# A two-layer network on one core: order of loads, pace of side work and place of the shared blocks

## Chip, cores and metric

The kernel runs on one core of a Trainium2 chip. The metric is the device time of one execution, in microseconds.

## What is computed

The input is x, 8 sequences of 256 tokens with 256 features, all in fp32. Four sublayers follow each other, each with a residual and a layer norm (weights without scale or shift):

```
x = norm(x + attention(x))        # 16 heads of 128, causal
x = norm(x + moe0(x))             # 32 experts, width 96, the 6 best by sigmoid score, weights normalized,
                                  # plus a shared expert of width 192
x = norm(x + ssm(x))              # gated state space layer: in-projection, causal convolution of 4 taps,
                                  # 8 heads of 64, state 64, RMS norm, out-projection
x = norm(x + moe1(x))             # 16 experts, width 176, in 4 groups: the 2 best groups, then the 4 best experts,
                                  # softmax scores, normalized; plus a shared expert of width 352
out = x
```

An expert computes (silu(x Wg) * (x Wu)) Wd for the tokens that chose it, and the results are added with their weights.

## The kernel before

The 2048 tokens are 16 tiles of 128. The tiles are handled in four quads of four tiles (`q`) and in two halves of eight (`h`). The layers of experts are called L0 (moe0) and L1 (moe1). The SSM works on "pairs" `p` of two sequences, which are the same four tiles as a quad.

**The stream.** After attention, everything hangs on one list of blocks, `STREAM` (lines 98 to 108). A block is 128 rows times one expert. Routed blocks (line 95) read rows from a DRAM table `xs`, in which each token's row was scattered to a place sorted by expert; there are 79 of them per half in L0 and 47 in L1, enough for any choice. Shared blocks (line 90) are two per tile and read the rows from SBUF. The list before the change is: L0 shared 0 to 31, L0 half 0 at 32, L0 half 1 at 111, L1 shared of tiles 0 to 7 at 190, L1 half 0 at 206, L1 shared of tiles 8 to 15 at 253, L1 half 1 at 269, the end at 316. Every engine has a loop over n through this list, and places its other work by n, in program order. An engine executes in order, so whatever is placed at n stands in the way of what is placed later.

- TensorE (line 1614): at n it turns the rows of block n+2 (`block_turn`, two transposes of `xb`), does gate and up of block n+1 (`block_gate_up`) and down of block n (`block_down`).
- ScalarE (line 853): copies the turned rows to `xbT` (n+2), silu of the gate (n+1), copies the output of block n to `b_out` (routed) or `acc` (shared).
- VectorE (line 1258): `b_act`, the product of gate and up, of n+1 (line 1111 for L0, 1106 and 1107 for L1), then everything that is not blocks.
- SyncE (line 544): issues loads and stores. `block_load` (line 495) waits until the slot of `bw` is free (a ring of 8 for L0 and 4 for L1, which counts `b_down_done`), issues the weights (line 505), waits until the rows' slot is free (a ring of 4, `xb_turned`), and issues the rows (line 511). It is called for block n+4 in L0 and n+3 in L1. `block_store` (line 513) writes two blocks of `b_out` to the DRAM table `os`, once the second is copied.
- GpSimd: `scatter` (line 611) has one indirect DMA per tile and choice (24 for a quad of L0, 16 for one of L1); `gather` (line 628) has one per choice of a tile (6 or 4) into the ring `og` of two tiles, and waits for the combine of the tile two before. It also multiplies `mix` for the SSM (line 644) and adds squares (line 650).

**Slots.** The SSM for the tokens of one half, and the choosing of L1's experts, run beside the blocks of the next stretch. `SPAN` (line 156) has two stretches of the stream: L0 half 1 (79 blocks), and L1 shared plus L1 half 0 (63 blocks). `slots_at` (line 159) spreads 90 slots v evenly over each. Pair i of the stretch starts at slot `FRONT[i]`, and a step of its plan has a number o = v - FRONT[i]: norm statistics at -3, turning of the normalized tile for pair 0 at -2, projections from 0, head products at 15 to 29 (they wait for `mix`, line 1545), out-projection at 33 and 35, gating of L1 at 43, choice at 44, its rank at 45, places at 46, scatter at 48; the table of block rows for the half at 48 and 49 of pair 1.

**Gathering and combining.** L0's result of a half is gathered and added to x in the next stretch: tile j at slots 0 to 4 and 13 to 28 (`mix_slot`, `gather_slot`, lines 167 to 174). `combine` (line 1088) adds the shared part and then one scaled row per choice (line 1095). It must be done before the norm of its quad. L1's half 0 is combined during L1's half 1 (`tail_mix`, line 180); half 1 is combined after the last block (lines 1348 to 1353), each quad followed by its norm and its store.

**Weighing.** `weights` (line 1050) computes for a quad the normalized weights (lines 1063 to 1067), the rows to gather (1070 to 1076), and the weight of each choice (1079 to 1085), in one piece of VectorE's program.

## Time and profile before

| what | value |
|---|---|
| runs | 1993.6, 1988.36, 1995.99 us; median 1993.6 |
| profiled execution | 1995.88 us, span 1994.2 us |
| granted TensorE clock, mean | 0.876 |
| PE busy | 1511.0 us (76%) |
| DVE, ACT, POOL busy | 975.6, 759.6, 442.1 us |
| DMA | 331.71 MB, mean 166 GB/s |

The span is the time from the first to the last instruction in the profiled execution; what lies around it is 1.7 us. Busy times are sums over the whole span, and they hide that the kernel has stages with different limits: attention until about 670, the shared blocks of L0 until 786, L0's first half until 954, its second half with the SSM of pairs 0 and 1 until 1284, L1's shared blocks and first half with pairs 2 and 3 until 1664, shared blocks until 1734, L1's second half until 1932, and the tail. The stages were told apart by VectorE's `b_act` instructions, one for each block. A wait is put down to the engine whose event came last; "issue" and "remote" (on the chain: "another core or an unknown queue") mean that the profile shows nothing that was waited for.

### The profile page before, as it was taken

Reading aid. Unit: us, or ns where it says so; the run is one execution under the profiler, and the core shown is the slowest. Engines: PE = TensorE matmul, PEld = TensorE weight load, DVE = VectorE, ACT = ScalarE, POOL = GpSimd, SP = SyncE. Lnnn points to the kernel's source line nnn. Section 1 sums busy time; section 2 is a strip of 40 time slices with the busy share of each in tenths; the row PEclk is TensorE's granted clock in tenths of the full one; section 3 lists DMA queues with packets and bytes.
Section 4 is the critical chain, followed back from the end, with each engine's and each line's share of the span. In section 5 each row is a group of like instructions: output and inputs, shape, how many; then the busy total and the mean of one; then the engine's idle time right before and its main releaser. Section 6 shows DMA issues by size and latency. Waiting matters only on the chain.

```text
span 1994.2 us, 30357 instructions
## 1 busy us (share of the span) xinstructions
PE 1511.0 (76%) x9344; PEld 1256.6 (63%) x9344; DVE 975.6 (49%) x3299; ACT 759.6 (38%) x2327; POOL 442.1 (22%) x422
## 2 busy tenths in 40 slices
PE   7999999999973418788457977827898787877760
PEld 6998898898873317667336766615666565655540
DVE  5777777777773302411336562425855333243315
ACT  5565565555530104345243543304344232223320
POOL 1010100000006470000515134261511503122015
PEclk9999999999986658799779988868998897888885
DMA  8265256246002142699637575421755664177743
GB/s 314 113 244 188 71 225 241 69 173 242 1 1 92 59 146 60 201 301 309 210 119 252 165 219 187 141 82 60 244 164 183 219 196 144 59 251 229 229 154 94
DMA packets 173078, 331.71 MB, mean 166 GB/s; under 512 B 17280, under 2 KB 85888, under 8 KB 171680
## 3 DMA queue, kind: packets, MB, share of 16 engines
q1 hardware_dynamic: 157600, 288.31, 43.4%
q0 software_dynamic: 15360, 41.96, 6.5%
q8 instruction: 58, 0.95, 0.2%
q14 instruction: 60, 0.49, 0.1%
HBM read 196.41 MB, written 133.27 MB: 165 GB/s over the span
## 4 chain that ended last, share of the span: by engine, by line
PE 45%; DVE 15%; issue 10%; DMA 8%; another core or an unknown queue 8%; ACT 7%; POOL 4%; SPq 2%; DVEq 0%; ACTq 0%; POOLq 0%
PE psum L407 37%; DMA xb<-xs 8%; PE psum L1579 2%; POOL xs L618 2%; POOL og L633 2%; PE psum L1401 1%; ACT p_sb L730 1%; DVE x L1095 1%; PE psum L1550 1%; SPq L505 1%; DVE s_sb L1123 1%; PE psum L1412 1%; DVE stats L940 1%; ACT p_sb L728 1%
## 5 line engine op out<-in xcount | busy, mean ns | idle before, releaser
L407 PE MATMUL psum<-xbT,bw 128*96 128x128 f32 (+1 forms) x2392 | 338.6, 293 | 0.0
L407 PEld LDWEIGHTS psum<-xbT,bw 128*96 128x96 f32 (+1 forms) x2392 | 312.8, 194 | 0.6 <-issue 0.3
L633 POOL DMA_INDIRECT og<-l_os,l_back_of x160 | 161.4, 1009 | 575.0 <-DMA l_os<-b_out 310.1
L407 PE MATMUL psum<-bw,b_act 96*128 96x256 f32 (+2 forms) x692 | 229.1, 424 | 63.9 <-ACT b_out L803 20.0
L1111 DVE TENSOR_TENSOR b_act<-psum,b_gated 96x128 f32<-96x128 f32 x190 | 53.9, 286 | 370.4 <-ACT b_gated L790 338.5
L618 POOL DMA_INDIRECT xs<-x,row_of x160 | 159.9, 1000 | 236.3 <-DVE row_of L1026 189.4
L1106 DVE TENSOR_TENSOR b_act<-psum,b_gated 128x128 f32<-128x128 f32 x126 | 36.7, 291 | 343.0 <-ACT b_gated L787 298.4
L779 ACT ACTIVATE xbT<-psum 128x256 f32<-128x256 f32 x252 | 96.3, 382 | 249.1 <-PE psum L1579 230.1
L407 PEld LDWEIGHTS psum<-bw,b_act 96*128 96x128 f32 (+2 forms) x692 | 113.6, 206 | 103.5 <-issue 75.9
L407 PE MATMUL psum<-l_shared_w,b_act 128*128 128x256 f32 (+1 forms) x192 | 70.9, 467 | 128.4 <-DVE b_act L1111 50.1
L1579 PE MATMUL psum<-ident,xb 128*128 128x128 f32 x504 | 110.2, 302 | 75.6 <-DMA xb<-xs 71.1
L1579 PEld LDWEIGHTS psum<-ident,xb 128*128 128x128 f32 x504 | 64.7, 151 | 140.4 <-DMA xb<-xs 101.8
L583 POOL TENSOR_TENSOR aw_lo<-aw_raw,aw_hi 128x512 fp32r<-128x512 f32 x32 | 41.2, 1289 | 484.0 <-ACT aw_hi L696 484.0
L803 ACT ACTIVATE b_out<-psum 128x256 f32<-128x256 f32 x252 | 96.8, 384 | 130.7 <-PE psum L407 125.8
L728 ACT ACTIVATE p_sb<-s_sb,neg_max 128x128 f32<-128x128 f32 x128 | 51.7, 404 | 210.8 <-DVE neg_max L1123 210.8
L790 ACT ACTIVATE b_gated<-psum 96x128 f32<-96x128 f32 x190 | 51.9, 274 | 194.1 <-PE psum L407 101.8
L407 PEld LDWEIGHTS psum<-l_shared_w,b_act 128*128 128x128 f32 (+1 forms) x192 | 34.1, 222 | 145.0 <-issue 58.5
L786 ACT ACTIVATE b_gated<-psum 128x128 f32<-128x128 f32 x126 | 35.0, 277 | 231.2 <-PE psum L407 181.8
L1095 DVE SCALAR_TENSOR_TENSOR x<-og,l_mix_of,x 128x256 f32<-128x256 f32 x160 | 79.7, 498 | 67.6 <-DMA og<-l_os,l_back_of 61.5
L407 PE MATMUL psum<-xT_hi,aw_hi 128*128 128x512 f32 x256 | 103.5, 404 | 10.5 <-POOL aw_lo L583 10.2
L407 PE MATMUL psum<-xT,l_shared_w 128*128 128x128 f32 (+1 forms) x640 | 102.2, 317 | 0.0
L407 PE MATMUL psum<-xT_hi,aw_lo 128*128 128x512 f32 x256 | 101.6, 397 | 0.0
(217 smaller groups left out, 3706.8 us busy)
## 6 DMA issues: line engine op xcount, KB each, us to landing
xs<-zeros SPq DMA_DIRECT2D x42, 1792.0 KB, 17.3
bw<-l_w SPq DMA_DIRECT2D x94, 640.0 KB
bw<-l_w SPq DMA_DIRECT2D x158, 320.0 KB
xb<-xs SPq DMA_DIRECT2D x252, 128.0 KB
l_os<-b_out SPq DMA_DIRECT2D x124, 256.0 KB
decay_all<-decay_dram SPq DMA_DIRECT2D x32, 384.0 KB
aw_raw<-attn_w SPq DMA_DIRECT2D x8, 1024.0 KB, 6.9
xs<-x,row_of POOLq DMA_INDIRECT x160
```

Of the source, the lines that this page charges most:

```text
L407: last = nc.tensor.matmul(out_ap, w, m, start=start and n == 0, stop=stop and n == len(pairs) - 1, **kw)
L583: pool.tensor_tensor(aw_lo[:, w], aw_raw[:, w], aw_hi[:, w].bitcast(F32), ALU.subtract).then_inc(aw_split, 1)
L618: pool.indirect_dma_start(xs[q // 2], bass.IndirectOffsetOnAxis(ap=row_of[:, t, k:k + 1], axis=0), x[:, t, :], None) \
L633: pool.indirect_dma_start(og[:, i % MIX_RING, k, :], None, os[f["layer"]][t // HALF_TILES], bass.IndirectOffsetOnAxis(ap=back_of[f["layer" ...
L728: act.activation(p_sb[:, u % 3, 0:P], s_sb[:, u % 2, 0:P], ACT.Exp, bias=neg_max[:, u % 3, 0:1], scale=-1.0, accum_out=row_sum[:, u % 3, 0:1])
L779: act.activation(xbT[:, r % 2].rearrange("p c t -> p (c t)"), psum[:, TURN_BANK, 0:DC * BLOCK], ACT.Copy).then_inc(xbT_ready, 1)
L790: act.activation(b_gated[h, n % 2, 0, :], psum[h, gu_bank(n), 0:P], ACT.Silu).then_inc(b_gated_ready, 1)
L803: act.activation(to, psum[:, DOWN_BANK, 0:D], ACT.Copy).then_inc(b_copied, 1)
L1095: ins = dve.scalar_tensor_tensor(x[:, t, :], og[:, i % MIX_RING, k, :], mix_of[f["layer"]][:, t, k:k + 1], x[:, t, :], ALU.mult, ALU.add)
L1106: dve.tensor_tensor(b_act[:, n % 2, 0, :], psum[:, gu_bank(n), P:2 * P], b_gated[:, n % 2, 0, :], ALU.mult)
L1111: dve.tensor_tensor(b_act[h, n % 2, 0, :], psum[h, gu_bank(n), P:2 * P], b_gated[h, n % 2, 0, :], ALU.mult).then_inc(bt_ready, 1)
L1579: last = pe.transpose(psum[:, TURN_BANK, c * BLOCK:(c + 1) * BLOCK], xb[:, r % XB_RING, c * P:(c + 1) * P], ident[:])
```

## The change

- **Loads.** `block_load` is cut in two. `LOADS` says at which n each is issued: weights for block n+6 in L0 and n+3 in L1, rows for block n+6, with exceptions at the start of a half. At one n, rows stand before weights, and both before the store. Sizes and numbers of the rings stay.
- **Slots.** 102 slots in place of 90, the pairs start at 18 and 50 in place of 8 and 40, and the second stretch ends 8 blocks before L1's second half (55 blocks). Gathers of L0 are placed two per slot, `combine` of L0 in two parts of three choices, in slots of their own; the scatter of L1 for pairs 0 and 2 is placed one DMA per slot (16 slots), for pairs 1 and 3 it stays in one piece. The steps of choosing L1's experts are placed in slots of their own (choice 45, rank 46, places 47, and for the table 48 to 51).
- **Weighing** is cut into three functions at three consecutive blocks.
- **The last 16 shared blocks** of L1 stand at the end of the stream. The new list is: L1 half 0 at 206, L1 half 1 at 253 (`TAIL`), L1 shared of tiles 8 to 15 at 300 to 315. L1's half 0 is combined at TAIL + 8 + 5j, tiles 8 to 11 of half 1 at the shared blocks 5, 8, 10 and 12; tiles 12 to 15 after the last block as before.

The operations themselves, their number and their shapes stay the same. Cut to what matters:

```diff
@@ the stream and its slots
-    if _f is L1:
-        FIRST["shared", _h] = len(STREAM)
-        STREAM += shared_blocks(L1, range(HALF_TILES * _h, HALF_TILES * (_h + 1)))
+    if (_f, _h) == (L1, 0):
+        FIRST["shared", 0] = len(STREAM)
+        STREAM += shared_blocks(L1, range(HALF_TILES))
     FIRST[_f["layer"], _h] = len(STREAM)
     STREAM += routed_blocks(_f, _h)
+FIRST["shared", 1] = len(STREAM)
+STREAM += shared_blocks(L1, range(HALF_TILES, TILES))
...
-FRONT = 8, 40
-SLOTS = 90
-SPAN = (FIRST[0, 1], FIRST["shared", 0]), (FIRST["shared", 0], FIRST["shared", 1])
+FRONT = 18, 50
+SLOTS = 102
+SPAN = (FIRST[0, 1], FIRST["shared", 0]), (FIRST["shared", 0], FIRST[1, 1] - 8)
...
-def mix_slot(j):
-    return 1 + j if j < QUAD else 16 + 4 * (j - QUAD)
-def gather_slot(j):
-    return max(0, mix_slot(j) - (1 if j < QUAD else 3))
+GATHERED = 0, 3, 6, 9, 18, 21, 27, 31
+COMBINED = (4, 5), (7, 8), (10, 11), (13, 14), (25, 26), (28, 29), (32, 34), (37, 38)
...
-    return TAIL + 2 + 4 * j
+    return TAIL + 8 + 5 * j if j < HALF_TILES else FIRST["shared", 1] + (5, 8, 10, 12)[j - HALF_TILES]
+
+def load_at(n):
+    f, h, m, _ = STREAM[n]
+    first = FIRST[f["layer"], h]
+    if f is L0:
+        weights = first - 5 if h == 0 and m < L0_RING - 1 else n - 6
+    else:
+        weights = first - 5 if h == 0 and m < L1_RING else n - 3
+    return weights, max(n - 6, first - 4 + m // 2)
+
+LOADS = {}
+for _n in ROUTED:
+    for _kind, _at in zip(("weights", "rows"), load_at(_n)):
+        LOADS.setdefault(_at, []).append((_kind, _n))
+
+def weigh_at(f, q):
+    return FIRST[0, 0] + 4 + 4 * q if f is L0 else TAIL + (1, 4, 10, 15)[q]
@@ SyncE: block_load is cut into weights_load (row, wait for the slot, bw) and rows_load (wait for the ring, xb)
-            for n in range(-4, BLOCKS + 1):
-                for lead, f in ((4, L0), (3, L1)):
-                    if 0 <= n + lead < BLOCKS and is_routed(n + lead) and STREAM[n + lead][0] is f:
-                        block_load(n + lead)
+            for n in range(BLOCKS + 1):
+                for kind, b in LOADS.get(n, ()):
+                    if kind == "rows":
+                        rows_load(b)
+                for kind, b in LOADS.get(n, ()):
+                    if kind == "weights":
+                        weights_load(b)
...
-                    if n == tail_mix(QUAD * q + 6):
+                    if n == tail_mix(QUAD * q + 3) + 5:
                         store(q)
@@ GpSimd: scatter takes a part, gather a range of k
-                        if v == gather_slot(j):
-                            gather(L0, HALF_TILES * h + j)
+                        if 0 <= v - GATHERED[j] < 3:
+                            k = 2 * (v - GATHERED[j])
+                            gather(L0, HALF_TILES * h + j, (k, k + 1))
...
-                        if o == 48:
+                        if i == 0 and 48 <= o < 64:
+                            scatter(L1, p, o - 48)
+                        if i and o == 48:
                             scatter(L1, p)
-                if n == TAIL:
+                if n == tail_mix(0) - 3:
                     all_stored(L1, 0)
                 for j in range(HALF_TILES):
-                    if n == tail_mix(j) - 2:
-                        gather(L1, j)
+                    if n == tail_mix(j) - 3:
+                        gather(L1, j, range(L1["top"]))
@@ VectorE: weights is cut into weights_sum, rows_back, weights_of; combine takes a range of k
-                for q in range(QUADS):
-                    if n == FIRST[0, 0] + 4 + 4 * q:
-                        weights(L0, q)
-                    if n == (FIRST["shared", 1] + 2 + 4 * q if q < 2 else TAIL + 4 * q):
-                        weights(L1, q)
+                for f in LAYERS:
+                    for q in range(QUADS):
+                        if n == weigh_at(f, q):
+                            weights_sum(f, q)
+                        if n == weigh_at(f, q) + 1:
+                            rows_back(f, q)
+                        if n == weigh_at(f, q) + 2:
+                            weights_of(f, q)
...
-                        if v == mix_slot(j):
-                            combine(L0, HALF_TILES * h + j)
+                        for part in range(2):
+                            if v == COMBINED[j][part]:
+                                combine(L0, HALF_TILES * h + j, range(3 * part, 3 * part + 3))
...
                             gate_read(L1, p)
                             gate_groups(L1, p)
+                        if o == 45:
                             choose(L1, p)
-                        if o == 46:
+                        if o == 47:
                             slots(L1, p)
-                        if i and o == 48:
+                        if i and o == 49:
                             table(L1, h)
-                        if i and o == 49:
+                        if i and o == 51:
                             rows_read(L1, h)
...
-                for j in range(HALF_TILES):
+                for j in range(HALF_TILES + QUAD):
                     if n == tail_mix(j):
-                        combine(L1, j)
+                        combine(L1, j, range(L1["top"]))
...
             for q in range(2, QUADS):
-                for t in range(QUAD * q, QUAD * (q + 1)):
-                    combine(L1, t)
+                if q == QUADS - 1:
+                    for t in range(QUAD * q, QUAD * (q + 1)):
+                        combine(L1, t, range(L1["top"]))
@@ TensorE
-                        if o == 45:
+                        if o == 46:
                             rank(L1, p)
-                        if i and o == 47:
+                        if i and o == 48:
                             count(L1, h)
-                        if i and o == 49:
+                        if i and o == 50:
                             rows_turn(L1, h)
```

## Rows read from the trace of the kernel before

**Rows 1.** The page's chain that ended last, shares of the span by engine

```profile
PE 45%; DVE 15%; issue 10%; DMA 8%; another core or an unknown queue 8%; ACT 7%; POOL 4%; SPq 2%; DVEq 0%; ACTq 0%; POOLq 0%
```

**Rows 2.** Windows: busy us (instructions) by engine, granted clock, DMA share, GB/s

```profile
794.00:844.00 50.00, 34.94 (x196) 31.03 (x196) 26.65 (x101) 15.87 (x50) 0.00 (x0) 0.80 0.64 204
844.00:954.00 110.00, 93.09 (x685) 78.48 (x684) 16.40 (x58) 56.46 (x172) 0.00 (x0) 1.00 0.94 303
954.00:1018.00 64.00, 20.96 (x106) 16.85 (x106) 20.28 (x60) 7.89 (x24) 34.92 (x36) 0.62 0.54 169
1018.00:1284.00 266.00, 216.22 (x1262) 171.28 (x1261) 137.56 (x375) 119.84 (x286) 73.41 (x51) 0.92 0.60 188
1284.00:1356.00 72.00, 24.77 (x101) 17.97 (x100) 24.23 (x75) 4.58 (x16) 47.17 (x49) 0.61 0.31 95
1356.00:1664.00 308.00, 265.57 (x1425) 194.03 (x1424) 160.42 (x418) 119.41 (x286) 72.00 (x55) 0.92 0.54 175
1664.00:1734.00 70.00, 54.47 (x278) 39.98 (x277) 20.74 (x93) 13.19 (x45) 21.63 (x23) 0.83 0.29 95
1734.00:1932.00 198.00, 148.99 (x825) 111.97 (x823) 64.93 (x228) 59.78 (x184) 22.74 (x24) 0.89 0.69 222
1932.00:1994.20 62.20, 1.30 (x4) 0.59 (x4) 29.30 (x88) 0.62 (x2) 31.32 (x32) 0.52 0.30 91
```

**Rows 3.** Waits of PE, 1734 to 1932: total us, times, longest us

```profile
PE psum L1579 <- DMA xb<-xs: 47.8, 30, 3.4
```

**Rows 4.** The page's DMA issues: count, KB each

```profile
bw<-l_w SPq DMA_DIRECT2D x158, 320.0 KB
xb<-xs SPq DMA_DIRECT2D x252, 128.0 KB
l_os<-b_out SPq DMA_DIRECT2D x124, 256.0 KB
```

**Rows 5.** Waits of PE, 794 to 844

```profile
PE psum L407 <- DVE b_act L1111: 13.9, 4, 3.8
```

**Rows 6.** Groups of DVE, 794 to 844: busy us, mean ns, idle before them

```profile
L1083 DVE TENSOR_TENSOR hits<-hits,weight 128x192 f32<-128x192 f32 x16 | 4.7, 352 | 0.1
L1079 DVE TENSOR_TENSOR hits<-place,places 128x192 f32<-128x192 f32 x16 | 4.6, 351 | 0.0
L1111 DVE TENSOR_TENSOR b_act<-psum,b_gated 96x128 f32<-96x128 f32 x17 | 4.5, 285 | 23.1 <-ACT b_gated L790 23.0
L1085 DVE TENSOR_REDUCE l_mix_of<-hits 128x24 f32<-128x768 f32 x4 | 3.8, 953 | 0.1
```

**Rows 7.** Groups of POOL, 954 to 1018

```profile
L633 POOL DMA_INDIRECT og<-l_os,l_back_of x36 | 34.9, 970 | 224.8 <-DMA l_os<-b_out 214.1 <-issue 10.7
```

**Rows 8.** Timeline of DVE: start us, us, instruction, idle before

```profile
969.22 3.09 DVE L1095 SCALAR_TENSOR_TENSOR x<-og,l_mix_of,x 128x256 f32<-128x256 f32 x6 [9.51 <-DMA og<-l_os,l_back_of]
```

**Rows 9.** Timeline of ACT, two of its pauses in bursts of POOL

```profile
1009.57 0.28 ACT L790 ACTIVATE b_gated<-psum 96x128 f32<-96x128 f32 x1 [19.97 <-remote]
...
1685.15 0.28 ACT L786 ACTIVATE b_gated<-psum 128x128 f32<-128x128 f32 x1 [12.25 <-remote]
```

**Rows 10.** Waits of PE, 1018 to 1284

```profile
PE psum L1550 <- POOL mix L648: 20.7, 2, 16.0
```

**Rows 11.** Waits of PE, 1356 to 1664

```profile
PE psum L1550 <- POOL mix L648: 12.5, 1, 12.5
...
PE psum L1579 <- DMA xb<-xs: 5.6, 6, 2.2
```

**Rows 12.** Timeline of POOL, a gather among DVE's scans

```profile
1072.04 2.26 POOL L633 DMA_INDIRECT og<-l_os,l_back_of  x1
```

**Rows 13.** Timeline of ACT, the last routed block's copy

```profile
1933.71 0.38 ACT L803 ACTIVATE b_out<-psum 128x256 f32<-128x256 f32 x1 [1.48 <-PE psum L407]
```

**Rows 14.** Timeline of DVE in the tail, first tile combined

```profile
1943.89 2.05 DVE L1095 SCALAR_TENSOR_TENSOR x<-og,l_mix_of,x 128x256 f32<-128x256 f32 x4 [11.46 <-DMA og<-l_os,l_back_of]
```

**Rows 15.** Timeline of DVE in the tail, last layer norm

```profile
1985.18 1.41 DVE L940 BATCH_NORM_STATS2 stats<-x 128x6 f32<-128x256 f32 x4
```

More of the change, by code:

```diff
@@ L609, in _, with scatter @@
             low_part(GROUPS - 1, 3)
[L611 to L619 removed]
+            def scatter(f, q, part=None):
+                if part in (None, 0):
+                    if f["layer"] == 0 and q == 0:
+                        pool.wait_ge(xs_zeroed, 16 * ZEROED * (GROUPS - 1))
+                    pool.wait_ge(placed, QUADS * f["layer"] + q + 1)
+                rows = [(t, k) for t in range(QUAD * q, QUAD * (q + 1)) for k in range(f["top"])]
+                for t, k in rows if part is None else rows[part:part + 1]:
+                    pool.indirect_dma_start(xs[q // 2], bass.IndirectOffsetOnAxis(ap=row_of[:, t, k:k + 1], axis=0), x[:, t, :], None) \
+                        .then_inc(scattered[q], 16)
             def all_stored(f, h):
@@ L626, in all_stored, with gather @@
                 pool.wait_ge(weighed, QUADS * f["layer"] + 2 * h + 2)
-            def gather(f, t):
+            def gather(f, t, ks):
                 i = f["layer"] * TILES + t
-                wait(pool, combined, i - MIX_RING + 1)
-                for k in range(f["top"]):
+                if ks[0] == 0:
+                    wait(pool, combined, i - MIX_RING + 1)
+                for k in ks:
                     pool.indirect_dma_start(og[:, i % MIX_RING, k, :], None, os[f["layer"]][t // HALF_TILES],
@@ L1097, in combine @@
                         chained(ins)
[L1098 to L1099 removed]
+                if ks[-1] == f["top"] - 1:
+                    ins.then_inc(combined, 1)
+                    dve.wait_ge(combined, i + 1)
             def block_act(n):
```

54 lines of the change are left out of this document (30 added, 24 removed).

## The prediction

> **What bounds it now.** I read the chain of waits first, then the span cut into the kernel's own stages, then who waits in each. On the chain PE has 45%, and 18% lies with "issue" and an unnamed queue [rows 1]: the kernel is PE-bound in places and idles in others. The stages say where [rows 2]. L0's first routed half has a start (794 to 844, DMA share 0.64) and a steady part (844 to 954: 58 blocks, one DVE instruction each, so 1.90 us a block, at DMA share 0.94 and 303 GB/s). The two state-space stretches each open with a hole, 954 to 1018 (PE busy 21 of 64) and 1284 to 1356 (25 of 72), and then run at a PE share of 0.81 and 0.86. L1's second routed half takes 198 us with PE busy 149, and 47.8 of the 49 idle microseconds are waits for `xb` [rows 3]. The 16 shared blocks ahead of it take 70 us, and after its last block PE does nothing for 60 us while gathers and combining run.
>
> **Rows ahead of weights.** Before, `xb` of block n+3 (L1) or n+4 (L0) is issued right behind the same block's weights. For L1 it is issued when down(n-1) has ended and wanted by the turn after down(n): one block of lead. After, rows are asked for 6 blocks early, bounded by the ring of four, so when turn(n+2) is done: four blocks of lead. Weights of L1 keep their lead of 3, but now stand behind the wait for that turn and one more DMA issue, some 1 us later. They are wanted two blocks on. A cycle of 198/46 = 4.3 us with one block of lead says that asking, landing and turning take about 4.3 us; (4.3 + 1)/2 = 2.7 us a block is then what weights allow, under what PE needs (149/46 = 3.2, part of it at the lower clock). The stage moves 198 x 222 = 44 MB, 145 us at 303 GB/s. So PE's 149 plus 7 for the two layer norms and for weighing that moves into this stage: 156, **-42**. Ends: -49 (no idle left), and -12 if weights take over most of the wait.
> In L0's first half the queue has little to give. 794 to 954 moves 10.2 + 33.3 = 43.5 MB [rows 2], 576 KB a block [rows 4]. At 303 GB/s that is 144 us, at the rate of a full share (303/0.94 = 322) 135; I take 141 of 160, **-19**, of which the earlier rows give the few us above 303 GB/s and the next part the rest. By the Trainium skill (DMA: Bandwidth & Descriptors, Specifications) one core's HBM limit is some 358 GB/s, by which an estimate would be 122 us; the trace disagrees, since a share of 0.94 gives 303.
>
> **Choosing in parts.** Weighing of a quad of L0 held DVE and cost PE 13.9 us in four waits [rows 5], and then some blocks at a lower clock. In three parts the longest is the last, (4.6 + 4.7 + 3.8)/4 = 3.3 us [rows 6]; DVE has 23.1/17 = 1.4 us free a block and one block of lead, so about 1 us of wait is left a quad. That lets DMA set the pace from 794 on: counted above.
>
> **The two openings.** SSM work of slot FRONT-2 needs four tiles combined and normalized. POOL issues a gather per (34.9 + 10.7)/36 = 1.27 us [rows 7]; the first tile is on DVE at 969.22 [rows 8], the next each six gathers (7.6 us) later, so the fourth is there at 992. Nothing in the change makes that faster: POOL doesn't wait for slots. What changes is what PE does beneath. Turning for pair 0 moves from slot 6 of 90 over 79 blocks (the 6th or 7th block) to slot 16 of 102 (the 13th): six more blocks at PE 93/58 = 1.6 us are done in the hole, 10 us. Splitting `combine` lets a block's b_act between the halves, and the chain reaches its end some 7 us earlier: **-17**. In the second opening the turn goes from the 4th block to the 9th: 5 shared blocks of 2.8 us (54.5 us busy at clock 0.83 is 45 at full, over 16) are 14, and 3 for the split: **-17**. Ends for both together: 0 and -60 (half of 43 + 47 idle, and all of what ACT loses below). In these bursts of POOL's indirect DMAs ACT stands idle with no releaser named, 19.97 us in one piece [rows 9]. Since the 36 gathers stay in one run, I leave those stalls where they are.
>
> **Scatter in parts.** Pair 0 and pair 2 scatter 16 times in a row, and PE waits for a `mix` behind them: 16.0 us and 12.5 us at the longest [rows 10, 11]. One scatter a slot leaves a mix waiting for one at most: **-15 and -14**. Against it: beside DVE's scans an indirect DMA took 2.26 us [rows 12], against 0.97 alone [rows 7], and 16 of those are 21 us more of POOL, spread over 16 slots of about 3 us, where it is idle two thirds of the time; no charge. The Trainium skill (SBUF, State Buffer; "two separate sides") says that GpSimd and DVE take a shared port pair as an exclusive lock, so that scatters amid DVE work would lengthen; the trace agrees, 2.26 against 0.97. Rows earlier in the L1 stage between 1356 and 1664: 5.6 us of `xb` waits [rows 11], **-5**; at best all the 42 us that PE idles there, at worst nothing.
>
> **More slots.** 102 slots over 79 and 55 blocks pack the same SSM work into fewer blocks, 1.29 and 1.85 slots a block instead of 1.14 and 1.43. The steps of choosing (rank, places, table) get slots of their own and are waited for by PE as before; I take nothing for them, under the blocks between. PE's work is the same and no DMA load is near its limit there (shares 0.60 and 0.54), so nothing, if PE is the limit. If it is not, see the last rival.
>
> **Shared blocks at the end.** Before: 70 + 62.2 = 132.2 us for the shared stage and the tail. After: L1's second routed half follows its own choosing directly. That ends 8 blocks ahead of block 253 (25 us), against 16 scatters at 1.27 (20 us) and their landing; SP's queue stands at block 249 until then, with weights of 252 and a store behind it. It fits by 2 us. What doesn't go is the stall in the burst, 12.25 us [rows 9]: **+12** kept. Tail, from the last routed copy at 1933.7: four gathers and their landing bring the first tile at 1943.9, +10 [rows 13, 14]. Combining stands at shared blocks 5, 8, 10, 12, that is at +15, +23, +30, +36 with 2.5 us each; the ring of two lets the gathers of tiles 12 and 13 go by +44. The 16 shared blocks end at +45. Then layer norm 5.6, tiles 12 and 13 (2.5 each) to +56; tile 14's gathers wait for tile 12's combine: 5 + 2.3, and tile 15's end 5 later, +64; combine 2.5 and the last norm with its store, 9.0 (1985.18 to the end [rows 15]): +76.5. In sum 12 + 1.7 + 76.5 = 90, **-42**. Bounds: -54 without the stall, -15 if the scatters cover nothing (12 more) and shared blocks are slowed by combining (15).
>
> **Sum.** -42 - 19 - 17 - 17 - 15 - 14 - 5 - 42 = -171. The profiled execution took 1995.9 us (span 1994.2), 2.3 above the median of the three runs: 1995.9 - 171 = 1825, set against the median 1993.6 - 171 = 1823. I say 1824.
>
> **Rivals.**
> - *Weights take over the wait* (0.14). Same queue, ring of four unchanged. For: PE then waits at gate-up where it waited at the turn, and L0 is at its DMA limit already. Against: two blocks of lead against one. L1's half gives 12 in place of 42, L0's first 8 in place of 19: 1824 + 41 = 1865.
> - *The openings stay as they are* (0.10). The chain gathers, combine, norm is as long as before, and the unnamed stalls of ACT fall on the added blocks: 34 lost, and a second such stall of 12 at block 249: 1870.
> - *The stalls without a releaser go too* (0.05): openings -50 in place of -34, no 12 at the scatter, L1 at -49: 1789.
> - *A slot has a price of its own* (0.03), slower. If DVE, ACT and POOL hand-offs set the time of a slot, not PE's work, the two stretches cost 330/90 = 3.67 and 380/90 = 4.22 us a slot, and 102 of each are 374 + 431, plus 8 bare blocks of 3.3: 831 in place of 710. With -42 - 19 - 42 elsewhere that is 2012. It decides above 3.86 us a slot; mine need 3.0. Against: PE is busy 0.81 and 0.86 behind the openings.
> - *Nothing comes of it* (0.02): SP, with rows standing before weights, waits for turns where it used to run ahead, and gives back at block 249 (252's weights) and in the SSM stretches what the turns gain: 1990.
>
> **Numbers.** The forecast has 0.66. All cases but the last two are faster: 0.95; same 0.02; slower 0.03 (0.5%, 10 us, is about what a measurement of this kernel tells from no change). The range holds the forecast with its own spread (about 25 either way), the first two rivals and most of the third: 1785 to 1880.
>
> **What would show it.** Waits of the turn for `xb` near nothing, and the DMA share in L1's second half near 0.9, with 3.3 us a block; if gate-up (`xbT,bw`) waits for weights there, the first rival holds. PE waits for `mix` of more than 3 us gone. Thirteen blocks done before pair 0's first turn. In the tail, under 35 us from the last shared block to the end. Wrong would be a slot of 3.9 us, or a hole of over 20 us at block 253.

## The result and the profile after

The changed kernel takes 1852.2 us, the median of four runs (1845.9 to 1856.4); beside it the kernel before took 1994.8 (four runs). The ratio is 0.9285, 95% interval 0.9247 to 0.9323: 143 us less, against 171 forecast, and inside the range. The sign and the order of size were right, and so were most terms; the openings, and the slots that were put at nothing, were not, and they make most of the 28 us that are missing.

From the top of the changed kernel's page: the span, the busy sums, and PE's and its clock's tenths in 40 slices:

```profile
span 1848.6 us, 30360 instructions
...
PE 1493.5 (81%) x9344; PEld 1240.5 (67%) x9344; DVE 995.6 (54%) x3299; ACT 751.7 (41%) x2326; POOL 448.7 (24%) x422
...
PE   7999999999997342688856888984689998798992
...
PEclk9999999999998655799987999995799999899996
```

PE's busy sum is nearly unchanged (1493.5 against 1511.0): the gain is idle time of PE. Where it went shows in the kernel's own stages. Windows of the changed kernel; they answer to [rows 2]:

```profile
core 0: us, PE busy (x) PEld busy (x) DVE busy (x) ACT busy (x) POOL busy (x), PEclk, DMA share, GB/s
794.00:936.00 142.00, 121.58 (x900) 108.12 (x899) 42.73 (x160) 66.83 (x225) 0.00 (x0) 1.00 0.96 313
936.00:1000.00 64.00, 34.72 (x180) 29.24 (x179) 22.14 (x67) 14.27 (x45) 35.16 (x36) 0.72 0.70 216
1000.00:1242.00 242.00, 207.83 (x1193) 160.24 (x1193) 150.00 (x380) 113.47 (x266) 78.23 (x54) 0.95 0.63 193
1242.00:1315.00 73.00, 33.74 (x148) 23.94 (x148) 19.63 (x51) 6.25 (x22) 41.05 (x44) 0.68 0.37 119
1315.00:1600.00 285.00, 245.17 (x1311) 179.06 (x1311) 171.51 (x438) 113.21 (x266) 93.84 (x72) 0.93 0.59 182
1612.00:1769.00 157.00, 140.29 (x842) 102.95 (x840) 74.44 (x280) 59.80 (x186) 30.39 (x32) 0.97 0.88 292
1769.00:1817.00 48.00, 42.27 (x244) 30.81 (x242) 18.19 (x51) 11.29 (x38) 23.17 (x24) 0.93 0.27 80
1817.00:1848.60 31.60, 2.37 (x4) 1.00 (x4) 19.90 (x69) 0.38 (x1) 7.88 (x8) 0.50 0.21 67
```

The steady part of L0's first half now moves 313 GB/s at a share of 0.96. The first opening (936 to 1000) has PE busy 35 of 64 us where it was 21. The second (1242 to 1315) has hardly changed: 34 of 73 against 25 of 72. L1's second routed half (1612 to 1769) took 157 us with PE busy 140, at a granted clock of 0.97, where it had 198 and 149. From the last routed block to the end are 48 + 32 us.

Who PE waits for in L1's second half, as in [rows 3]:

```profile
engine line waited for: us in total, times, longest us
PE psum L426 <- issue: 7.0, 13, 1.5
PE psum L426 <- ACT xbT L815: 5.1, 7, 1.1
PE psum L426 <- DVE b_act L1155: 4.5, 2, 2.7
```

`xb` is gone from the list, and no wait for weights stands in its place. For the second opening the same view names something else:

```profile
PE psum L426 <- ACT acc L839: 33.0, 2, 21.4
PE psum L426 <- issue: 6.2, 2, 4.9
```

I cut each trace by the times of `b_act`, of which every block has one, so that a stage is the same work in every kernel. Two columns (runs 9 and 10 explain them) are from another chip:

```
stage, us (by b_act)        before  after | before  after | forecast
                            the chips     | a chip with-  |
                            shown so far  | out pauses    |
L0 shared blocks             115.4  125.2 |  62.1   61.2  |    0
L0 half 0                    169.0  148.3 | 167.1  150.1  |  -19
L0 half 1 + SSM 0,1          330.4  305.4 | 315.1  293.9  |  -17 -15
L1 shared 0-7 (opening)      123.2  115.5 | 111.8   94.6  |  -17
L1 half 0 + SSM 2,3          256.5  254.9 | 253.8  249.8  |  -14 -5 +12
L1 half 1                    198.1  156.7 | 202.0  162.4  |  -42
L1 shared 8-15                67.6   48.1 |  49.8   41.4  |  } -54
tail                          62.5   31.6 |  61.5   31.7  |  }
```

### The profile page after: what moved, and what is told of

It is laid out like the page before. It is cut to its first block, busy times and chain, and to the rows that moved or that the text cites. A ratio compares the mean times of both kernels' runs of the same rounds, so it can differ in the third digit from the quotient of the medians.

```text
span 1848.6 us, 30360 instructions
## 1 busy us (share of the span) xinstructions
PE 1493.5 (81%) x9344; PEld 1240.5 (67%) x9344; DVE 995.6 (54%) x3299; ACT 751.7 (41%) x2326; POOL 448.7 (24%) x422
## 4 chain that ended last, share of the span: by engine, by line
PE 49%; DVE 17%; another core or an unknown queue 10%; issue 9%; ACT 7%; DMA 5%; POOL 2%; SPq 1%; DVEq 0%; ACTq 0%; POOLq 0%
PE psum L426 40%; DMA l_os<-b_out 4%; PE psum L1633 2%; DVE x L1142 2%; PE psum L1455 2%; ACT p_sb L766 1%; DVE s_sb L1171 1%; PE psum L1604 1%; PE psum L1466 1%; DVE conv L1256 1%; DVE stats L976 1%; DVE x L990 1%; ACT p_sb L764 1%; ACT kT_hi L742 1%
## 5 line engine op out<-in xcount | busy, mean ns | idle before, releaser
L426 PE MATMUL psum<-xbT,bw 128*96 128x128 f32 (+1 forms) x2392 | 325.7, 285 | 13.0 <-issue 6.8
L426 PEld LDWEIGHTS psum<-xbT,bw 128*96 128x96 f32 (+1 forms) x2392 | 298.5, 186 | 18.9 <-issue 11.2
L426 PE MATMUL psum<-bw,b_act 96*128 96x256 f32 (+2 forms) x692 | 222.6, 413 | 72.3 <-ACT b_out L839 27.1
L650 POOL DMA_INDIRECT xs<-x,row_of x160 | 165.6, 1035 | 221.0 <-DVE row_of L1062 176.3
L426 PEld LDWEIGHTS psum<-bw,b_act 96*128 96x128 f32 (+2 forms) x692 | 107.8, 196 | 115.5 <-issue 74.8
L1633 PE MATMUL psum<-ident,xb 128*128 128x128 f32 x504 | 106.1, 293 | 5.6 <-ACT xbT L815 4.7
L1142 DVE SCALAR_TENSOR_TENSOR x<-og,l_mix_of,x 128x256 f32<-128x256 f32 x160 | 87.5, 547 | 27.4 <-DMA og<-l_os,l_back_of 22.2
L426 PEld LDWEIGHTS psum<-xT,l_shared_w 128*128 128x128 f32 (+1 forms) x640 | 92.7, 212 | 13.4 <-issue 10.8
## 6 DMA issues: line engine op xcount, KB each, us to landing
xs<-zeros SPq DMA_DIRECT2D x42, 1792.0 KB, 17.4
```

The lines of the kernel that those rows point to most:

```text
L426: last = nc.tensor.matmul(out_ap, w, m, start=start and n == 0, stop=stop and n == len(pairs) - 1, **kw)
L650: pool.indirect_dma_start(xs[q // 2], bass.IndirectOffsetOnAxis(ap=row_of[:, t, k:k + 1], axis=0), x[:, t, :], None) \
L1142: ins = dve.scalar_tensor_tensor(x[:, t, :], og[:, i % MIX_RING, k, :], mix_of[f["layer"]][:, t, k:k + 1], x[:, t, :], ALU.mult, ALU.add)
L1633: last = pe.transpose(psum[:, TURN_BANK, c * BLOCK:(c + 1) * BLOCK], xb[:, r % XB_RING, c * P:(c + 1) * P], ident[:])
```

## The experiments

The first four runs shared a chip; the changed kernel's 1852.2 us is the time to hold them against. It was measured beside a kernel before of 1994.8 us and these beside 1998.5, so some 4 us of every such difference of totals are open; the stages don't depend on it. Behind each median stands in brackets that of the kernel before on the same chip.

**1. Loads issued as before.** `LOADS` is not used; both loads of a block stand together, weights first.

```diff
-                for kind, b in LOADS.get(n, ()):
-                    if kind == "rows":
-                        rows_load(b)
-                for kind, b in LOADS.get(n, ()):
-                    if kind == "weights":
-                        weights_load(b)
+                for lead, f in ((4, L0), (3, L1)):
+                    b = n + lead
+                    if b < BLOCKS and is_routed(b) and STREAM[b][0] is f:
+                        weights_load(b)
+                        rows_load(b)
```

> The changed kernel with the loads placed as before: block n+4 (L0) and n+3 (L1), weights and right behind them the rows. Theory (rows asked for one block ahead of their use set the pace of L1's half, and a part of L0's first half): L1's second half goes from 157 us back to about 198, L0's first half from 148 to about 155, together +50: about 1900 us against 1852 of the changed kernel. Rival (the gain of those stages comes from other edits, such as the shared blocks leaving and weighing in parts): within 10 us of 1852.

Measured: 1918.6 us (1998.5), ratio 0.957 (0.953 to 0.962), so this part alone is worth some 66 us. L1's second half is 211.8 us, L1's first half 268.6 (+14), L0's first half 154.8 (+6.5). PE's wait for `xb` in L1's second half, 1629 to 1840:

```profile
PE psum L1632 <- DMA xb<-xs: 47.4, 30, 3.4
```

The 47.8 us of `xb` of [rows 3] are back, as 47.4. The half costs more than in the kernel before (211.8 against 198.1) although these waits are the same: PE is busy 155.6 us in it, at a granted clock of 0.87, against 149.3 at 0.89, and it has 8.6 us of other waits. It also holds the weighing of quads 0 and 1 now; the two layer norms were in it before. In L1's first half the waits for `xb` are 14.3 us, in seven, against 5.6 in the kernel before [rows 11], and that is the loss of 14 us. That PE comes to the turns at other times with 102 slots in 55 blocks may be why they are longer; it wasn't tested.

**2. Rows after weights, with the lead kept.** The two loops over `LOADS` change places.

> The changed kernel with the order at each block turned round: weights first, then rows; the rows are still asked for six blocks early. Theory (it is the lead that counts, four blocks in place of one, and not which of the two goes first): within 8 us of 1852. Rival (rows that stand behind weights land late whatever the lead): waits for xb come back in L1's second half and the time is 1870 to 1890.

Measured: 1843.3 us (1998.5), ratio 0.922 (0.919 to 0.926); the changed kernel's is 0.9285. The lead counts, and the order named first in the change is no gain: the other way round is 9 us faster, most of it in L0's first half (139.9 against 148.3). I had allowed 8 us either way. In the windows of that half the queue is fuller with weights first: 336 GB/s at a share of 0.99 (794 to 927), where the changed kernel has 313 at 0.96. Why the order does that isn't known.

**3. Shared blocks 8 to 15 back in front of L1's second half.** The rest as changed; combining of the second half falls behind the last block again, and the slots end 8 blocks ahead of the shared blocks.

```diff
-    if (_f, _h) == (L1, 0):
+    if _f is L1:
...
-FIRST["shared", 1] = len(STREAM)
-STREAM += shared_blocks(L1, range(HALF_TILES, TILES))
```

> The changed kernel with L1's shared blocks of tiles 8 to 15 back ahead of L1's second half, and tiles 8 to 11 combined after the last block. Theory (the shared blocks cover the tail's gathers at the end, and cover little in the middle): +45 us, 1897. Rival (in the middle they cover the scatter and its stalls, so that the gain is half of that): +25, 1877.

Measured: 1877.1 us (1998.5), ratio 0.939 (0.937 to 0.942), 25 us more. The rival had the number. The tail is 62.9 us again, +31; but the shared blocks take 41.9 us in the middle where the kernel before needed 67.6. The choosing ends 8 blocks before them, as in the changed kernel, so the burst of scatters and its pause fall on the routed blocks ahead. Of what the move and the earlier choosing give together, 25 is the move.

**4. Scatter of pairs 0 and 2 in one piece.**

```diff
-                        if i == 0 and 48 <= o < 64:
-                            scatter(L1, p, o - 48)
-                        if i and o == 48:
+                        if o == 48:
                             scatter(L1, p)
```

> The changed kernel with L1's scatters of pairs 0 and 2 in one piece of 16 again. Theory (PE waits for mix behind them, 16 and 12.5 us): a wait of PE for POOL's mix of 12 to 16 us comes back in each of the two stretches, +29, 1881. Rival (the wait is only moved, and in one piece the scatters cost less of POOL): within 8 us of 1852.

Measured: 1887.3 us (1998.5), ratio 0.945 (0.941 to 0.950): 35 us more, 20 in L0's second half, 16 in L1's first. PE's waits there, 940 to 1260 and then 1376 to 1648:

```profile
PE psum L1602 <- POOL mix L681: 19.4, 2, 17.8
...
PE psum L1602 <- POOL mix L681: 19.1, 2, 17.4
```

17.8 and 17.4 us in one piece, where the kernel before had 16.0 and 12.5 [rows 10, 11]. The term stands, and was a little too small. The charge that the prediction named and left out, 21 us of POOL for 16 scatters beside DVE's scans, came as 5 and 6: three of each 16 took 2.25 to 2.28 us, and the 16 together 20.5 and 21.6 us in the changed kernel, where 16 undisturbed ones take 15.4.

Runs 5 to 8 came on another chip, on which the kernel before took 1854.5 us, not 1995, and runs 9 to 11 on a third with 1843.0. So between chips I compare ratios and stages, not times. The changed kernel itself didn't run beside runs 5 to 8; put together from the stages that they leave alone, it would take 1706 us there.

**5. Weighing in one piece again** (`weights_sum`, `rows_back` and `weights_of` of a quad at one n; in L1 too, whose second half took 158.0 us, as in runs 7 and 8).

> L0's weighing of a quad back in one piece, its blocks as in the changed kernel. My theory (weighing held DVE, and PE beneath it, by 13.9 us in four waits [rows 5], and with rows ahead DMA sets the pace of that stage): the start of L0's first routed half is up to 12 us longer, 1852 + 5 to 12. Rival (DMA alone sets the stage's pace, share 0.96 in the changed kernel's trace, so a wait of PE for DVE is given back at once): within 3 us of 1852.

Measured: 1716.6 us (1854.5), ratio 0.9265 (0.923 to 0.930). L0's first half took 163.7 us; in the two other kernels on the same chip that leave it as changed (runs 6 and 7) it took 152.5 and 151.9, so 11 to 12 less. PE's waits for `b_act` here, 678 to 842, and in the changed kernel (run 9), 681 to 831:

```profile
PE psum L426 <- DVE b_act L1159: 14.1, 4, 4.0
```
```profile
PE psum L426 <- DVE b_act L1159: 1.9, 4, 0.8
```

14.1 us in four waits is the 13.9 of [rows 5]. They are not given back, although DMA's share is 0.95 over the half. About half of the loss is PE's clock: it is busy 136.0 us in the half at a granted 0.94, and 129.4 at 1.00 in run 7. By the ratios alone the loss doesn't show: 0.9265 here, 0.9246 for the changed kernel in run 9, each within the other's interval; it rests on the stage. With run 1's 6.5 that makes some 18 of this half's 17 to 21 us: one third is the loads, two thirds the weighing in parts.

**6. The openings as before** (FRONT 8, 40; SLOTS 92; six gathers of a tile in one slot, `combine` in one slot).

> The shape of both openings as before (8 and 40 slots in front, 92 slots, a tile's gathers and its combine in one slot), the rest as in the changed kernel. If the openings gave what I forecast (17 each): 1852 + 34 = 1886. Rival (only the first opening gave anything; in the second the hole stayed, 142 us to the first turn of pair 2 less what the first opening gave): 1852 + 8 to 17, 1860 to 1869, with L1's shared blocks 0 to 7 and first half as long as in the changed kernel to 5 us.

Measured: 1731.1 us (1854.5), ratio 0.933 (0.930 to 0.937). Against the kernels on the same chip that leave these stages as changed (runs 5 and 8), L0's second half is 300.4 us to their 297.8 and 296.0, and the L1 stretch 115.2 + 242.2 = 357.4 to their 343.7 and 344.6. So the openings are worth 3 to 4 and 13 us, 17 of the 34 forecast. (The total is 25 above the 1706: 7 more lie in L1's second half, 164.5 us against 158, where the waits are no longer but PE is busy 145.2 us at a granted 0.93 against 137.6 at 0.98. Whether that has to do with the openings isn't shown; the changed kernel has 162.4 us there in run 9, at 0.96.) The rival of this run was wrong too: the second opening does gain, and more than the first, on a chip where nothing pauses.

**7. Pair 1's scatter later.** It stood at its slot 48, with 16 DMAs ahead of the second opening's gathers.

```diff
+                    if h and v == 12:
+                        scatter(L1, 1)
...
-                        if i and o == 48:
+                        if p == 3 and o == 48:
                             scatter(L1, p)
```

> The scatter of pair 1 in L1's opening (28 DMAs of POOL in a row with the gathers behind it) is moved behind the first four gathers of the choosing. Theory A (the second opening ends when the gathers of pair 2 are through POOL's queue, 16 scatters of 1.27 us ahead of them are 20 us, and their burst holds the signals of PE): first turn of pair 2 up to 20 us earlier, 1832 to 1845. Theory B (the hole is PE's late signals in any burst, and POOL's queue is not the bound): the pauses only move, within 4 us of 1852.

Measured: 1694.7 us (1854.5), ratio 0.914 (0.912 to 0.917). The opening's stage took 82.4 us against 94.6 in runs 5 and 8, and L1's first half 245.6 against 249.1 and 250.0. That is theory A: POOL's queue holds the second opening. It gave 12 there, of the up to 20 us expected.

**8. L0's scatters of quads 2 and 3 spread over the first routed half.**

```diff
-            for q in range(QUADS):
+            for q in range(2):
                 scatter(L0, q)
...
+            for j in range(2 * QUAD * L0["top"]):
+                q, part = 2 + j // (QUAD * L0["top"]), j % (QUAD * L0["top"])
+                pool.wait_ge(b_down_done, 12 + 19 * j // 10 + 1)
+                scatter(L0, q, part)
```

> L0's scatters of quads 2 and 3 (48 of 96 in one run, under L0's first routed half) are spread, one for every 1.9 blocks from block 12 on. Theory A (what PE's increments of semaphores wait for is a dense run of POOL's indirect DMAs; ACT's unnamed pauses of 12.5, 21.3 and 24.9 us between 690 and 754 are waits for those): the pauses in that stretch go, L0's first routed half is 148 - 30 = 118 us by PE's blocks, but DMA's share of 0.96 allows less: some 135, so 1815 to 1840. Theory B (the pauses have to do with the number of indirect DMAs, or with the DMA load, not their density): pauses stay, spread over the half, within 5 us of 1852 or slower.

Measured: 1705.4 us (1854.5), ratio 0.918 (0.915 to 0.922). This says nothing on its question: the trace of this chip holds no pause that it could have taken away. L0's first half took 156.1 us where runs 6 and 7 took 152: spreading costs 4 where nothing pauses. What it would do on a chip with pauses stays open.

**9 and 10. The changed kernel and the kernel before, once more.**

> The changed kernel once more, unaltered, beside the kernel before. The last four kernels ran on a chip where the kernel before takes 1854 us and their traces hold no pause without a releaser over 4 us. Theory (the pauses belong to the chip, or to its condition, and the change's parts have their price without them): on such a chip 1706, put together from stages that those four left as they were; on one like the first, 1852. Rival (the pauses come and go from run to run on one chip): times that differ by over 50 us within this kernel's own runs.

> The kernel before once more, for its trace. Theory (pauses belong to the chip): on a chip that takes 1854 us the trace holds none of ACT's unnamed pauses of 12 to 25 us, and the 140 us less than 1994 lie within runs of POOL's indirect DMAs: about 56 in L0's shared stage (as 62 against 125 us in the other kernels), the rest in L0's first half, the two openings and the scatters; stages without such runs are as long as before to 3 us. Rival (a slower chip throughout, the clock or the memory): the difference is spread over all stages in proportion, 7% each.

Measured: 1705.4 us for the changed kernel (1843.0), ratio 0.9246 (0.918 to 0.931), and 1843.2 for the kernel before in its one profiled run. 1706 had been put together from stages. The kernel before took 1994.8, 1998.5 and (in the last run below) 1998.9 on some chips and 1854.5 and 1843.0 on others, and on each chip its runs agree to 25 us. Its stages without pauses stand in the table above: up to L0's shared blocks 618.3 us against 671.3 (-53), in them 62.1 against 115.4 (-53), L0's second half -15, the second opening -11, shared 8 to 15 -18; L0's first half -2, L1's first and second half -3 and +4, tail -1. Nearly all of the 152 us lies in stages in which POOL issues indirect DMAs in long runs, as expected; it is not spread. The first 53 are the end of attention, which the expectation didn't name: L0's scatters begin there, at 603.

**11. Weights first and pair 1's scatter late, together.**

> Weights of a step asked for before its rows (their lead kept), and pair 1's scatter behind the first four gathers of the second opening. If both gains stand and add: 9 for the order and 16 for the later scatter (12 in the opening, 4 in the blocks before it): 25 below the changed kernel, 1681 on a chip without the pauses, 1827 on one with them. Rival (the scatter only moves its cost behind the opening, and the order is worth nothing outside one chip): within 5 us of the changed kernel.

Measured on the same chip as 9: 1674.8 us (1843.0), ratio 0.907 (0.902 to 0.913), against 1705.4: 31 us less than the changed kernel. The opening's stage is 82.1, L1's first half 243.8, L0's first half 145.5, L1's second half 155.1. In the changed kernel beside it these took 94.6, 249.8, 150.1 and 162.4. Both gains stand. It is the fastest kernel of the study, on a chip without pauses; on one with them it was not run.

**12. On top of that, the opening's combines 3 to 4 slots later.** In the timeline of DVE in the first opening of the changed kernel (run 9), DVE comes to the first combine long before the rows:

```profile
839.10 0.29 DVE L1159 TENSOR_TENSOR b_act<-psum,b_gated 96x128 f32<-96x128 f32 x1 [1.24 <-ACT b_gated L826]
839.30 0.41 DVE L1139 TENSOR_TENSOR x<-x,acc 128x256 f32<-128x256 f32 x1
849.66 1.55 DVE L1142 SCALAR_TENSOR_TENSOR x<-og,l_mix_of,x 128x256 f32<-128x256 f32 x3 [9.94 <-DMA og<-l_os,l_back_of]
851.24 0.29 DVE L1159 TENSOR_TENSOR b_act<-psum,b_gated 96x128 f32<-96x128 f32 x1
```

9.94 us idle at the head of the queue, and the `b_act` of the blocks behind it wait with it; PE waits 9.8 us for one of them.

```diff
-FRONT = 18, 50
-SLOTS = 102
+FRONT = 22, 54
+SLOTS = 106
...
-GATHERED = 0, 3, 6, 9, 18, 21, 27, 31
-COMBINED = (4, 5), (7, 8), (10, 11), (13, 14), (25, 26), (28, 29), (32, 34), (37, 38)
+GATHERED = 0, 3, 6, 9, 22, 25, 31, 35
+COMBINED = (7, 8), (11, 12), (14, 15), (17, 18), (29, 30), (32, 33), (36, 38), (41, 42)
```

> On top of the last kernel (weights first, pair 1's scatter later), the combining of an opening's first four tiles stands 3 to 4 slots later and SSM work 4 slots later (FRONT 22, 54; 106 slots), the gathers where they are. In both traces of the changed kernel DVE reaches the first combine 10 us (second opening 14 us) before its rows have landed, with the b_act of two blocks queued behind it, and PE waits for those: the split of combine didn't help there. Theory (blocks held behind the first combine are what is left of the opening): PE's longest wait for b_act in each opening falls from 9.8 and 14 us to under 5, and the time by 5 in each, 10 in all: a ratio to the kernel before of 0.902 where 0.9074 was measured, 1665 on a chip without the pauses. Rival (the chain gathers, combine, norm sets the end of the hole, and blocks done in it are missed as cover later, where slots come denser, 106 in the same blocks): within 4 us of the last kernel, with PE's wait moved from b_act to x or to the steps behind it.

Measured: 1859.5 us (1998.9), ratio 0.9285 (0.922 to 0.935), on a chip with pauses, so neither number of the expectation can be held against it. By stages against run 2, which has the same order of loads on such a chip: L0's second half is 296.7 us against 305.6, of which run 7 would give 4 to 5 to pair 1's scatter. PE's longest wait for `b_act` in that opening is 4.0, under the 5 of the theory, but run 2 has 1.1 there, so on such a chip it shows nothing. And the opening and the half behind it took 396.5 us against 370.6, and PE's longest wait in 1235 to 1360 is this:

```profile
PE psum L1490 <- DVE x L992: 31.5, 1, 31.5
```

31.5 us for the last tile's x: PE's wait has moved, as the rival has it, and become longer. But not by the rival's cause. DVE has combined the fourth tile by 1275.2, and then stands at a block's `b_act`, which waits for ACT's silu, with the norm queued behind it; timelines of DVE and ACT:

```profile
1272.12 3.12 DVE L1144 SCALAR_TENSOR_TENSOR x<-og,l_mix_of,x 128x256 f32<-128x256 f32 x6
1305.34 0.29 DVE L1156 TENSOR_TENSOR b_act<-psum,b_gated 128x128 f32<-128x128 f32 x1 [30.10 <-ACT b_gated L825]
```
```profile
1304.70 0.28 ACT L824 ACTIVATE b_gated<-psum 128x128 f32<-128x128 f32 x1 [26.92 <-remote]
```

So PE's wait is one of the pauses of the next section, and the number says nothing on the later combines. It begins in a run of 40 indirect DMAs (1249 to 1300), of which 16 are the scatter that run 11 moved there too. What run 11 would give with pauses, and run 12 without, stays open.

## What the pauses are

The unnamed stalls of ACT [rows 9] were the one thing that I could only keep or drop in the sum. In the changed kernel the second opening begins so; timeline of ACT, 1236 to 1275, then of PE:

```profile
1241.41 0.39 ACT L839 ACTIVATE b_out<-psum 128x256 f32<-128x256 f32 x1
1249.44 0.28 ACT L822 ACTIVATE b_gated<-psum 128x128 f32<-128x128 f32 x1 [7.65 <-remote]
...
1271.88 0.28 ACT L822 ACTIVATE b_gated<-psum 128x128 f32<-128x128 f32 x1 [21.88 <-remote]
```
```profile
1250.69 2.37 PE L426 MATMUL psum<-l_shared_w,b_act 128*128 128x256 f32 x4 [4.88 <-issue]
1252.99 2.93 PE L426 MATMUL psum<-xT,l_shared_w 128*128 128x128 f32 x12
```

PE's last gate-up starts at 1252.99 and takes 2.93 us. ACT, which waits here for one semaphore, moved by PE, takes it up at 1271.88, 16 us later. The same place in the changed kernel on a chip without pauses (there it begins at 1124):

```profile
1124.00 0.38 ACT L839 ACTIVATE b_out<-psum 128x256 f32<-128x256 f32 x1
1126.03 0.28 ACT L822 ACTIVATE b_gated<-psum 128x128 f32<-128x128 f32 x1 [1.64 <-PE psum L426]
...
1128.62 0.28 ACT L822 ACTIVATE b_gated<-psum 128x128 f32<-128x128 f32 x1 [2.04 <-PE psum L426]
...
1131.22 0.28 ACT L822 ACTIVATE b_gated<-psum 128x128 f32<-128x128 f32 x1 [1.15 <-PE psum L426]
```

Two shared blocks follow in steps of 2.6 us, and each time ACT's releaser is PE. The same can be asked of all 316 blocks: how long after the end of PE's gate-up, and of ACT's own instruction before it, does ACT start on that block? In the trace of the kernel before it is over 2 us in 11 blocks, 129 us in all, and in that of the changed kernel in 18 blocks, 167 us; every one of these delays begins inside a run of 8 or more indirect DMAs or less than 1 us behind it. In the traces of both kernels on the other kind of chip (runs 9 and 10) no block has one, though the runs of DMAs are just as long and dense (96 from 604 to 727 us, 1.28 us each). From ACT's silu to DVE's `b_act` no delay over 2 us stands in any of the four. So in these traces the pauses come only in such runs, and only on some chips. The records of semaphores are incomplete in the traces with pauses (DVE's `b_act` has 293 for 316 blocks in the kernel before), so they can't say where PE's signal was held up. What differs between the chips is not shown.

## Why the prediction was right, and where not

Where not said otherwise the numbers are those without pauses (right half of the table), since they show the parts clean; the total is nearly the same on both kinds of chip (137 and 143 us).

- *Rows ahead, L1's second half*: -42 forecast, -39.6 and -41.4 measured. Right, and by its own mechanism: no `xb` and no weights in PE's waits. That the stage's 156 came as 157 (on the chips of the forecast) is in part luck: PE was busy 140 and idle 17, where I had 149 and 7. The clock was granted at 0.97, 0.89 before [rows 2], and the time was lost again in short waits for ACT and unnamed ones. The 7 were also given for the wrong reason in part: the two layer norms stood in this half before, only the weighing moved in.
- *L0's first half*: -19, measured -17 and -21. Right, and in its parts too: I had given the loads the few us above 303 GB/s and the weighing the rest, and the runs put 6.5 on the loads and 11 to 12 on the weighing. My ends for the rate, 303 and 322 GB/s, held on the chips of the forecast (313 at a share of 0.96) but not as a rule: run 2 moved 336 there at 0.99, and without pauses the changed kernel moved 333 over the whole half at 0.99, so 303/0.94 was not the rate of a full share.
- *Scatter in parts*: -15 and -14; alone 20 and 16 (run 4). Right, a little small.
- *First opening*: -17, and 3 to 4 by undoing it. What failed is the step on splitting `combine`, which was to let a block's `b_act` between the halves and end the chain 7 us earlier. The blocks more in the hole came: 15 stand ahead of pair 0's first turn instead of 8, and PE's idle in the 64 us fell from 32 to 22. But the turn comes no earlier, 49.8 us after the half's first block against 47.6 before. DVE stands 9.94 us with the first half of the first combine at the head of its queue, as it stood 9.51 with the whole of it [rows 8], and no block gets past; and what the hole gives, the slots behind it give back in part (below).
- *Second opening*: -17. Without pauses the stage gave -17.2. With them it gave -7.7, since pauses took 11 us of that stage before (123.2 - 111.8) and 21 after (115.5 - 94.6): more blocks stand in the burst, and each needs PE's signals. That is what the rival "openings stay as they are" said of it, and it was right for that opening, on those chips. My text left those stalls where they are, and that was the step that failed there.
- *More slots: nothing.* This was the term mis-sized most, by some 15 us: L1's first half had -14 and -5 due, and gave -4. The waits of PE over the shared and routed blocks of this stretch, kernel before and changed one, without pauses:

```profile
PE psum L407 <- DVE b_act L1107: 27.9, 4, 14.6
PE psum L1434 <- DVE x L954: 15.2, 3, 11.3
PE psum L1550 <- POOL mix L648: 12.7, 2, 12.4
PE psum L407 <- DVE prefix L1007: 7.1, 2, 5.0
...
PE psum L1579 <- DMA xb<-xs: 4.5, 6, 2.5
...
PE psum L407 <- issue: 1.0, 1, 1.0
PE psum L1550 <- DVE y L1238: 1.0, 1, 1.0
```
```profile
PE psum L426 <- DVE b_act L1155: 19.0, 4, 14.0
PE psum L1488 <- DVE x L990: 12.5, 4, 6.9
PE psum L426 <- issue: 8.0, 6, 3.1
PE psum L1604 <- DVE y L1286: 6.3, 5, 2.1
...
PE psum L1588 <- DVE h_tok L1269: 3.6, 2, 2.2
PE psum L426 <- DVE prefix L1043: 1.4, 2, 1.2
PE psum L1604 <- POOL mix L681: 1.0, 1, 1.0
...
PE psum L1633 <- DMA xb<-xs: 0.6, 1, 0.6
```

`mix`, `prefix`, `xb` and `b_act` fell by 12, 6, 4 and 9 us; but waits for `y`, `h_tok` and unnamed ones rose from 2 to 18. I put this down to the same SSM work standing in 55 blocks in place of 63, which leaves PE less to do between a step and what it needs from DVE; no run gave the 8 blocks back alone, so that is argued, not shown. "Nothing, if PE is the limit" held the condition, and it isn't quite: PE is busy 0.89 there. The rival "a slot has a price" named the mechanism, and was wrong by far in size: at 3.4 us a slot, even with the 8 blocks without slots counted in ((94.6 + 249.8)/102), it stayed under the 3.86 at which it decides.
- *Shared blocks at the end* (-42): on the chips of the forecast the stretch from the last routed block took 79.7 us (48.1 + 31.6); I had 78.2 (76.5 and 1.7; the terms of the 76.5 as written add up to 75.5). The stall of 12 at the scatter burst came as 9.5, from 1578.9 to 1588.4, and in L1's first half. Right on both. Run 3 adds what the sum didn't separate: only 25 of the 50 us are the move's, the rest is the choosing's earlier end.

Of the rivals, weights didn't take over the wait, and "nothing comes of it" fell with every run. "The stalls go too" asked for the change to remove them; a chip did that, and the gain was no larger for it (137).

The sum by undoing parts one at a time is 66 + 35 + 17 + 25 + 12 = 155 against 143. It mixes totals with pauses and stages without them, so 12 us is not much of a difference; as far as it goes the parts overlap.

## What to carry to other kernels

A queue that is not full by share can still set the pace through its lead: two numbers of a stage, its cycle a block and the blocks of lead, told that its 48 us of waits would go. Splitting a step that waits helps only if the wait is not in its first part; ask what the head of an in-order queue waits for, and put it later instead (run 12 tried that, and doesn't tell). Packing side work denser seems to cost nothing only while the bounding engine has enough work between each step and its answer, which no run here tested alone; count the slots against blocks before calling it free. And a stage full of unnamed pauses should be compared on a second chip before its time is charged to the kernel.

## What the runs showed of the hardware

- The same program took 1995 us on some chips and 1843 to 1854 on others, steady within each. Each chip was used at one time only, so chip and moment aren't told apart. The stages that differ are those with long runs of GpSimd's indirect DMAs, in which signals come late, with pauses of up to 25 us on ACT in the changed kernel (728.9 to 753.8) and of 26.9 in run 12; the mean granted clock differs too (0.876 against 0.904 for the kernel before, 0.906 against 0.945 for the changed one).
- An indirect DMA in a run took 1.25 to 1.28 us of POOL's queue on both kinds of chip; on those with pauses the run of L0's 96 scatters is broken in two, 604 to 664 and 686 to 747, against 604 to 727 in one.
- Weights first get more out of a full queue than rows first. Windows of L0's first half, run 9 (rows first) and then run 11 (weights first), same chip:

```profile
722.00:831.00 109.00, 94.96 (x705) 84.54 (x704) 16.64 (x58) 51.60 (x174) 4.14 (x5) 1.00 0.99 325
```
```profile
722.00:826.50 104.50, 92.31 (x696) 83.05 (x696) 16.66 (x58) 52.70 (x175) 4.77 (x5) 1.00 1.00 341
```

325 GB/s at a share of 0.99, and 341 at 1.00. The Trainium skill (DMA: Bandwidth & Descriptors, Specifications) states an HBM limit of some 358 GB/s for a core; 341 is 5% short of it. But it doesn't bound what moved here: while L0's last 30 scatters ran beside the loads, the same two kernels moved 380 and 383 GB/s for 51 us (689 to 740), counting reads and writes, and there the measurement decides. Run 11:

```profile
689.00:740.00 51.00, 42.03 (x304) 36.65 (x303) 28.73 (x108) 22.73 (x77) 30.14 (x30) 1.00 1.04 383
```

So a DMA share of 1.00 is no rate by itself: it went with 325, 341 and, at 1.04, 383 GB/s.
